# Three gathered neighbour sums of a graph network as products with a matrix of edge counts in bf16

## The reference

```python
# 1, attention (8 relations, 4 heads):
feat = einsum('ni,rhid->rnhd', h, conv_weights)
e = leaky_relu(el[type, src] + er[type, dst], 0.2)     # per edge and head
alpha = softmax of e over the edges with the same dst
x += segment_sum(alpha[..., None] * feat[type, src], dst) + h_bias
# 2, GCN (10 clusters): degrees count the edges and one more self loop
logits = D^-1/2 (A + I) D^-1/2 ((h + sum(cluster_emb)) @ W) + bias
x += h + softmax(logits) @ cluster_emb
# 3, GIN: edge network, then an MLP 256 -> 1024 -> 1024 -> 256 with layer norms
e = relu(edge_attr @ ee_w1 + ee_b1) @ ee_w2 + ee_b2
# with self loops, whose attributes are zero
agg = segment_sum(h[src] + e, dst)
x += relu(ln(h + MLP((1 + eps) * h + agg)) * bn_g + bn_b)
# 4, SAGE: mean over the in-edges
h = relu(ln(ln-and-relu of x) * gamma + beta)
x += (segment_sum(h[src], dst) / max(deg, 1)) @ W_l.T + b_l + h @ W_r.T
```

## Time and profile before

| | us |
|---|---|
| median of 3 runs | 4173.94 (4170.83 to 4174.08) |
| the profiled execution | 4168.64 |
| its span | 4166.8 |

### The profile page before, as it was taken

The page is one execution under the profiler, slowest core; times in us unless marked ns, Lnnn a source line. Parts: engine busy times, 40 slices in busy tenths (PEclk is TensorE's granted clock), DMA queues, the critical chain, the costliest instruction groups (busy, mean ns, idle before and its releaser), DMA issues.

```text
span 4166.8 us, 59236 instructions
## 1 busy us (share of the span) xinstructions
PE 3273.9 (79%) x16728; PEld 2258.8 (54%) x16728; DVE 2326.6 (56%) x4971; ACT 1189.8 (29%) x3540; POOL 1989.6 (48%) x2014
## 2 busy tenths in 40 slices
PE   3898388888868888887788888899999973666666
PEld 3444255555545554454777777555555542665556
DVE  6788577777664444446555555444444456555444
ACT  1222377778721111112111111233333322000000
POOL 0000477777307777772777777100000004777774
PEclk6899699999958889886899999999999986777767
DMA  4344333434211111111344444100000003333333
GB/s 99 118 152 142 109 107 108 107 108 108 56 45 36 17 17 17 17 16 44 111 113 114 114 114 113 45 5 5 5 5 5 5 12 95 102 102 101 102 102 101
DMA packets 216469, 301.43 MB, mean 72 GB/s; under 512 B 122598, under 2 KB 162715, under 8 KB 212251
## 3 DMA queue, kind: packets, MB, share of 16 engines
q0 software_dynamic: 88000, 200.32, 18.1%
q1 hardware_dynamic: 124027, 67.66, 6.4%
q10 hardware_dynamic: 4320, 31.95, 1.9%
HBM read 255.85 MB, written 43.93 MB: 72 GB/s over the span
## 4 chain that ended last, share of the span: by engine, by line
POOL 35%; PE 30%; DVE 13%; issue 13%; DMA 4%; ACT 3%; DVEq 1%; SPq 1%; ACTq 0%; POOLq 0%
POOL BG L406 14%; POOL SL L406 13%; PE PS L897 12%; POOL BG L416 7%; PE PS L723 3%; DVE SUMS L1112 3%; PE PS L608 3%; PE PS L765 3%; PE PS L746 2%; PE PS L721 1%; DVE OHB L1119 1%; PE PS L761 1%; PE PS L786 1%; ACT SL L565 1%; DMA BG<-rel_d 1%
## 5 line engine op out<-in xcount | busy, mean ns | idle before, releaser
L1248 DVE TENSOR_TENSOR SUMS<-SUMS,PS 128x256 f32 (+1 forms) x1750 | 709.0, 415 | 988.0 <-PE PS L746 363.7
L416 POOL DMA_INDIRECT BG<-feat_d,IDXST x500 | 484.4, 969 | 501.2 <-DMA feat_d<-SUMS 349.2
L406 POOL DMA_INDIRECT SL<-h_d,IDXS x500 | 502.8, 1006 | 289.1 <-issue 149.2
L406 POOL DMA_INDIRECT BG<-h_d,IDXS x500 | 491.7, 983 | 152.3 <-issue 148.0
L897 PE MATMUL PS<-BG,SL 128*128 128x512 f32 (+1 forms) x1440 | 533.0, 527 | 26.6 <-ACT SL L565 26.6
L765 PE MATMUL PS<-OHB,SL 128*128 128x128 f32 x2000 | 339.7, 328 | 248.1 <-DMA SL<-h_d,IDXS 202.9
L515 ACT ACTIVATE BG<-BG,SL 128x64 f32<-128x64 f32 x2000 | 482.0, 335 | 0.0
L765 PE MATMUL PS<-OHB,BG 128*128 128x128 f32 x2000 | 340.4, 329 | 179.7 <-DMA BG<-h_d,IDXS 131.1
L765 PEld LDWEIGHTS PS<-OHB,SL 128*128 128x128 f32 x2000 | 310.6, 236 | 281.8 <-issue 181.8
L765 PEld LDWEIGHTS PS<-OHB,BG 128*128 128x128 f32 x2000 | 308.1, 236 | 215.4 <-DVE SUMS L1248 128.3
L897 PEld LDWEIGHTS PS<-BG,SL 128*128 128x128 f32 x1440 | 271.8, 192 | 261.7 <-issue 211.7
(11 more groups left out here) (232 smaller groups left out, 4229.4 us busy)
## 6 DMA issues: line engine op xcount, KB each, us to landing
feat_d<-SUMS ACTq DMA_DIRECT2D x30, 1040.0 KB, 4.5
BG<-rel_d SPq DMA_DIRECT2D x100, 160.0 KB, 3.1
AL<-in_edge_attr_dram SPq DMA_DIRECT2D x100, 128.0 KB
BG<-feat_d,IDXST POOLq DMA_INDIRECT x500, 2.8
SL<-h_d,IDXS POOLq DMA_INDIRECT x500
BG<-h_d,IDXS POOLq DMA_INDIRECT x500
h_d<-BG SPq DMA_DIRECT2D x8, 640.0 KB, 3.3
BG<-in_L_gnn_w_dram SPq DMA_DIRECT2D x1, 4096.0 KB, 20.4
```

The costliest lines, as they stand in the source:

```text
L406: pool.indirect_dma_start(SLOTS[t // 10 % 2][:, t % 10, 0:width], None, table, bass.IndirectOffsetOnAxis(ap=IDXS[:, t:t + 1], axis=0),).th ...
L416: pool.indirect_dma_start(RING[:, t // NB % 3, t % NB, :], None, table, bass.IndirectOffsetOnAxis(ap=IDXST[:, t:t + 1], axis=0),).then_inc ...
L1248: return tt(a, a, v, ALU.add)
```

## The change

The neighbour sums of layers 2, 3 and 4 are computed as products with a dense matrix of edge counts, a_d, in HBM (3,840 sources by 4,352 columns, bf16, 33.4 MB). Columns 512 and up are destinations. Column t below 512 takes the edges of tile t that go to its first destination, since these alone can be shared with the tile before; after a product DVE adds such a held column t to column `BASE[t]`.

1. *Counts.* Two edges of a tile with the same source and destination must be written as one count. In layer 1's loop PE turns a broadcast column of KEY (source times 4096 plus relative destination) into the free quarter of the tile's bank, and DVE compares it with KEY and sums the matches into MULT (one instruction more a tile on each). `added` is now incremented by this instruction.
2. *The matrix.* POOL clears ZRO, SP writes zeros over a_d in 30 DMAs, one for every 15 tiles of layer 1. After layer 1's loop POOL issues 499 scatters (`TR = T - 1`; the last tile is padding only), each of 128 two-byte elements, one behind the other with no wait between them. Their landings are counted in four semaphores, for which SP waits before the first load from a_d.
3. *Edge network.* It runs alone, between layer 2's rows and its product, over all 125 groups of four tiles, with its own double buffers.
4. *Product of layer 2.* The rows of y are split into three bf16 parts (30 columns together), stationary; a_d streams in 5 column groups of 1,024 (the last of 256) by 30 source tiles, through 7 slots.
5. *Products of layers 3 and 4.* h is split into three bf16 parts of 256; a step (group, source tile) has 12 matmuls of 512 columns, or 6 of 256 in the last group. ACT casts, DVE subtracts, five tiles at a time. Turns and layer 4's self product stand between the steps of the first group. h3_d and y_d are gone, h2_d stays for the residual of the MLP.
6. *Places.* The parts and slots lie in BG, AL, SL and HSF. W1 is loaded after the first product, W2, W3 and the bias rows after the second.
7. Many single-use semaphores are merged into `dve_mark` and `pe_mark`.

The diff, cut to its core:

```diff
@@ SP @@
+            sp.wait_ge(s("zero_ready"), 1)
+            for t in range(NT):
+                sp.wait_ge(s("agg_ps"), 20 + 15 * t)
+                load(rows(a_d, t).rearrange("p (a n) -> p a n", a=2), bc(ZRO.unsqueeze(1), [P, 2, AD // 2]), "a_zero")
...
+            def adjacency(p, g, t):
+                n, (c0, w) = adj(p, g, t), GROUPS[g]
+                if n >= NR:
+                    sp.wait_ge(s("a_used"), n - NR + 1)
+                load(AR[p][n % NR][:, 0:w], a_d[t * P:(t + 1) * P, c0:c0 + w], f"a_in{n % NR}")
...
+            for k in range(4):
+                sp.wait_ge(a_set[k], 16 * len(range(k, TR, 4)))
+            sp.wait_ge(s("dve_mark"), DVE_MARKS["y_ready"])
+            adjacency_from(0, 0, every)
+            adjacency_from(1, 0, NR)
+            sp.wait_ge(s("a_used"), every)
             load(W1S, w1.rearrange("(c p) n -> p c n", p=P), "mlp_in")
...
+            sp.wait_ge(s("a_used"), 2 * every)
+            load(BR[0], row(b1, P), "mlp_bias")
+            load(W2S, w2.rearrange("(c p) n -> p c n", p=P), "mlp_late")
+            for v, a in ((BR[1], b2), (B3R, b3), (GNR, bn_g), (BNR, bn_b)):
+                load(v, row(a, P), "mlp_bias")
             load(W3S, w3.rearrange("(c p) n -> p c n", p=P), "mlp_late")
@@ POOL @@
-            gather(2, y_d, K)
...
-            gather(3, h2_d, D)
...
-            gather(4, h3_d, D)
+            pool.wait_ge(s("a_zero"), 16 * NT)
+            pool.wait_ge(s("dve_mark"), DVE_MARKS["adj_ready"])
+            for t in range(TR):
+                pool.indirect_dma_start(
+                    a_d.rearrange("n (w o) -> (n w) o", o=1), bass.IndirectOffsetOnAxis(ap=IDXST[:, t:t + 1], axis=0),
+                    VAL[:, t:t + 1], None,
+                ).then_inc(a_set[t % 4], 16)
@@ PE @@
-                last.then_inc(s("agg_ps"), 1)
+                turn(PS[:, bank, 3 * P:4 * P], bc(KEY[:, n:n + 1], [P, P]), P).then_inc(s("agg_ps"), 1)
...
+            def adjacent(p, g, t, lhs):
+                w = GROUPS[g][1]
+                if t == 0 and g >= 2:
+                    pe.wait_ge(s("d_free"), p * len(GROUPS) + g - 1)
+                rhs = adjacency_here(pe, p, g, t)
+                for part in range(3):
                     for c in range(2):
+                        for o in range(0, w, 512):
+                            m = min(512, w - o)
+                            last = pe.matmul(PS[:, 4 * (g % 2) + 2 * c + o // 512, 0:m], lhs(t, part)[:, c * P:(c + 1) * P],
+                                             rhs[:, o:o + m], start=(t == 0 and part == 0),
+                                             stop=(t == NT - 1 and part == 2))
+                last.then_inc(s("a_used"), 1)
...
+            for v in range(NE):
+                for k in range(4):
+                    hidden_sum(v, k)
+                    if k == 0 and v + 2 < NE:
+                        net_turn(v + 2)
+                    if k % 2 == 1 and v + 1 < NE:
+                        hidden(v + 1, k // 2)
@@ DVE @@
                     add = tt(a, a, PS[:, AGG_BANKS[n % 4], 0:3 * P].rearrange("p (a n) -> p a n", a=3), ALU.add)
                     add._wait_ge(s("added"), n + 10)
-                    add.then_inc(s("added"), 1)
+                    ts(SAME[:, n % 2, :], PS[:, AGG_BANKS[n % 4], 3 * P:4 * P], KEY[:, n:n + 1], 0.0, ALU.is_equal, ALU.add,
+                       accum_out=MULT[:, n:n + 1]).then_inc(s("added"), 1)
...
+            def neighbours(p, into, held, banks):
+                for g, (c0, w) in enumerate(GROUPS):
+                    dve.wait_ge(s("a_used"), adj(p, g, NT - 1) + 1)
+                    v = banks(g)
+                    if g == 0:
+                        step(cp(held, v[:, :, 0:512]))
+                    o = 512 if g == 0 else 0
+                    a = into[:, :, c0 + o - 512:c0 + w - 512]
+                    step(tt(a, a, v[:, :, o:w], ALU.add))
+                    dve.engine_nop().then_inc(s("d_free"), 1)
+                    for n in range(GR * g, min(GR * (g + 1), TR)):
+                        if n % 10 == 0:
+                            base = bases(n, 10)
+                        a = into[:, :, bass.ds(base[n % 10], 1)]
+                        step(tt(a, a, held[:, :, n:n + 1], ALU.add))
```

More of the change, by code:

```diff
@@ new lines, in adjacency, with adjacency_from @@
+            def adjacency(p, g, t):
[3 more added lines that the diff above has]
+                load(AR[p][n % NR][:, 0:w], a_d[t * P:(t + 1) * P, c0:c0 + w], f"a_in{n % NR}")
+            def adjacency_from(p, first, last):
+                for g in range(len(GROUPS)):
+                    for t in range(NT):
+                        if first <= g * NT + t < last:
+                            adjacency(p, g, t)
@@ new lines, in self_product, with h3_part @@
+            def self_product(t):
+                pe.wait_ge(s("n3_ht"), t + 1)
+                if t >= 2:
+                    pe.wait_ge(s("n3_done"), t - 1)
+                for c in range(2):
+                    last = pe.matmul(PS[:, 6 + t % 2, 0:D], HTR[:, t % 2, c, :], WLR[:, 1, c, :],
+                                     start=(c == 0), stop=(c == 1))
+                last.then_inc(s("n3_ps"), 1)
+            def h3_part(t, part):
+                return HIMID[:, t, part, :] if part < 2 else LO[:, t, :]
@@ L1283, in _, with edge_one_hot, bases @@
-            dve.wait_ge(s("f0_den"), 1)
+            def edge_one_hot(v):
+                k = slice(4 * (v % 2), 4 * (v % 2) + 4)
+                tt(OH[:, k, :], bc(IOTA[:, :].unsqueeze(1), [P, 4, P]),
+                   bc(DREL[:, 4 * v:4 * v + 4].unsqueeze(2), [P, 4, P]), ALU.is_equal).then_inc(s("oh_ready"), 1)
+            def bases(first, n):
+                _, base = nc.values_load_multi_w_load_instructions(
+                    BASE[:, first:first + n], engines=[DVE], min_val=0, max_val=N,
+                    skip_runtime_bounds_check_because="clamped to N when it was computed")
+                return base
@@ new lines, in _ @@
+            dve.engine_nop().then_inc(s("ys_ready"), 1)
+            neighbours(0, ACC[0:K3, 1:2, :], VBK.unsqueeze(1),
+                       lambda g: PS[0:K3, 2 * (g % 2):2 * (g % 2) + 2, :].rearrange("p (c a) n -> p c (a n)", c=1))
+            dve.wait_ge(s("pe_mark"), PE_MARKS["f1_tp"])
+            for i in range(2):
+                step(dve.tensor_reduce(Z[:, 15 * i:15 * i + 15, :],
+                                       PS[:, 4 + i, 0:15 * K3].rearrange("p (t a k) -> p t k a", t=15, a=3), AX, ALU.add))
@@ L1324, in _ @@
+            step(tt(Z, Z, Y, ALU.add))
             step(tt(Z, Z, bc(DG[:, :].unsqueeze(2), [P, NT, K]), ALU.mult))
```

623 lines of the change are left out of this document (329 added, 294 removed).

## The result

The changed kernel took 3850.11 us (median of four runs, 3833.78 to 7338.08) where the kernel before took 4174.01 (4170.83 to 4177.25) beside it: ratio 0.921, 95% interval 0.918 to 0.924. On a further chip, in a later series, it took 3846.47 (3843.31 to 3850.89) against 4171.75, ratio 0.922 (0.920 to 0.923). One run in eight took 7338 us; it has no trace, nothing explains it, and it is left out of the ratio. The forecast was 3680 us with a range of 3600 to 3840: the direction was right, the time 170 us too short and 10 us outside the range.

The account below looks back on a forecast made before the run. Three of the four neighbour sums were taken as bound by POOL's issue of gathers, the MLP by TensorE. The terms summed to -497 us: 4168.6-497+5 = 3677, say 3680 us, range 3600 to 3840.

Parts of the forecast that it names:

- Attention sum: Layer 1's loop: the added comparison makes DVE the bound at 1.41 us a tile, +67 us, POOL's start +3.
- Between: Stretch after the attention sum: three small copies and larger memsets, +2 us on 104.
- Scatters and edge network: After the attention sum, side by side: 499 scatters at 1.31 us set the end at 658 us; edges take 495.
- rival 1: Scatters run at the pace of landing, 2.8 us each instead of 1.31: +744 us, 4421 us in all; chance 0.06.
- rival 2: Scatters at 1.5 to 2.2 us each; at 1.8, +245 us, 3925 us in all; chance 0.07.
- rival 5: Edges and scatters run one after the other, both asking DMA queues for small packets: +440 us, 4120; chance 0.01.
- GCN product: Layer 2's product after the scatters: DVE's 499 held adds and 50 fetches set the end, 154 us (140 to 200).
- Softmax on the clusters: The softmax takes one more reduction: +1 us.
- GIN product: Layer 3's product: 350 us instead of 686.4, -336, with loads and DVE's held adds hidden.
- MLP: W2 can load only after the product, so DVE waits for five bias rows: +14 us (5 to 20).
- SAGE product: Layer 4's product, from ACT's last pass over the rows: 387 us instead of 681, -294.
- Rival 3: Products slower than 0.215 us a pass, by PE's clock or weight loads: +116 us at clock 0.85, 3795; chance 0.08.

Follow-up runs that it names:

- run 3672: No follow-up run: 3672 us is the forecast for the changed kernel's profiled run, 4168.6-497, without the 5 us added for the median of the runs; measured 3850.
- the run with two parts: Changed kernel with the lowest of three bf16 parts left out of the GIN and SAGE products: 3778.93 us, ratio 0.906.
- the last version: Changed kernel plus GCN held columns on TensorE, spread pads, four scatters out at most, twenty bases a fetch, reordered GIN/SAGE work: 3652.71 us, ratio 0.876.
- four out: Changed kernel with each scatter waiting for the landing of the one four before it: 3838.71 us, ratio 0.920.
- the four variants that ran there: Changed kernel without GCN held adds (4389.66 us), with fixed columns (4404.58), with twenty bases a fetch (4483.96), without counting (4547.84).

## Why the prediction was right in direction and wrong in size

Forecast for the profiled run 3672, measured 3850: 178 us to place.

- *Attention sum*: forecast +70, measured +58 (1197.4 against 1139.6). VectorE was the bound, as said, though busy for 85% of the stage (88% from the first add on), not over 90. The counting by itself is worth 51 to 54 us. In the pair below the comparison starts 0.47 us after its add and the next add 0.39 after the comparison: the comparison was priced well (0.36), but the add no longer costs the 0.58 that five dependent ones took the earlier trace rows, since the comparison need not wait for it: 0.86 us a pair where I had 0.94. That is 40 us over 500 tiles, and the loop from the first add took 670 us, 1.34 a tile, where 1.41 makes 705. But the forecast counted its 1.41 us a tile from the stage's start with 3 us ahead of it, while the first add comes only 26 us in (500.8 to 526.9; it was 20 before). So -35 and +23 make the -12: the stage came out nearly right because two errors went against each other. The accumulator's read is an instruction of its own (the first two lines are the adds of all 500 tiles, before and after):

```profile
L1229 DVE TENSOR_TENSOR SUMS<-SUMS,PS x500: 525/555/558, 521.5 to 1139.0; 128x384 f32 x167
L1330 DVE TENSOR_TENSOR SUMS<-SUMS,PS x500: 524/554/559, 526.9 to 1196.6; 128x384 f32 x167
...
1191.83 0.56 DVE L1330 TENSOR_TENSOR SUMS<-SUMS,PS 128x384 f32 x1
1192.30 0.34 DVE L1332 TENSOR_SCALAR_CACHE_REDUCE SUMS<-PS,SUMS 128x128 bf16<-128x128 f32 x1
1192.57 0.08 DVE L1332 DVE_READ_ACCUMULATOR SUMS<-PS,SUMS 128x1 f32 x1
1192.69 0.56 DVE L1330 TENSOR_TENSOR SUMS<-SUMS,PS 128x384 f32 x1
```

- *Between*: forecast +2, but the scatters, not this stretch, are on the path: -2.
- *Scatters and edge network*: 1.304 us a scatter (forecast 1.31), 499.5 us for the edges (495), both side by side and nothing of rivals 1, 2 and 5 on this chip. From the end of the last to the first load: 18 us, not 2.8, by the pads' one address, so 670.5 instead of 658: +12.
- *GCN product*, the step that failed: "499 held columns one by one ... I take 0.20, plus 50 fetches of bases at 0.45". Measured from the first load it is 266.8 us (1867.9 to 2134.7) instead of 154, +113: the adds 499 x (0.29-0.20) = 45, the fetches 50 x (1.72-0.45) = 64 (of each gap of 1.86, 0.14 belong to the add), the rest 4. The mechanism (VectorE sets the end) was right; both prices were wrong, and the range of 140 to 200 too narrow. The rows were misread twice. The pace of dependent instructions in the earlier trace rows was of fixed addresses, and the adds at a register's address in the same group stood at 0.38 for 0.28 long, so 0.10 from end to start: with 0.148 of length that is 0.25, nearer to the truth than the value I took. And the 0.87 us before L1203 was halved for half as many bases, though nothing in the trace said that a fetch scales; the runs show a fixed part, and ten bases cost twice what I had read for twenty. The row itself was typical (22.6 us of idle time in all 25 fetches of that loop, 0.90 each); why twenty bases stop VectorE for 1.53 us between the held adds is open.
- *Softmax on the clusters*: 48.3 against the forecast 46.6: +2.
- *GIN product*: forecast 350, measured 384: +34. A step is 2.59 us and the clock 1.0 in the middle groups, as forecast. What was called hidden was not: VectorE's held adds (73 us a group in the run with two parts, 2352.6 to 2426.0, not 37) leave 49 behind the last full group, so it ends 8 us after TensorE (2559.3, 2567.4). And in the first group TensorE stood 3.5 us at each block of five rows, waiting for ScalarE's last cast, as VectorE's second difference was queued behind five turned tiles that wait for TensorE. I had counted casts only ahead of the product. Behind three of these five waits, and in the group's first step, the granted clock was down too (0.50, which is 1.2 GHz, to 0.66), and a step took up to 5.3 us instead of 2.75, some 7 us in all. The tail of 8, the waits of 18 and these 7 make 33 of the 34 (below, the row with a colon is the busy time of one such step, with the clock third from its end).

```profile
2213.60 4.45 PE L859 MATMUL PS<-AL,BG 128*128 128x512 bf16 x12 [3.52 <-ACT BG L590]
...
2233.02 2.76 PE L859 MATMUL PS<-BG 128*128 128x512 bf16 x11 [3.52 <-ACT BG L590]
...
2270.19 5.30 PE L859 MATMUL PS<-AL,BG 128*128 128x512 bf16 x12 [3.53 <-ACT BG L590]
...
2270.20:2275.60 5.40, 5.40 (x14) 2.17 (x15) 1.49 (x1) 1.27 (x1) 0.00 (x0) 0.50 0.01 3
...
2564.02 2.62 DVE L1383 TENSOR_TENSOR SUMS<-SUMS,OHB 128x2 f32 x9 [2.48 <-issue]
2566.67 0.69 DVE L1377 TENSOR_TENSOR SUMS<-SUMS,PS 128x512 f32<-128x512 f32 x1
```

- *MLP*: forecast +14, measured 829.8 against 815.3 (2637.8 to 3453.1): right, with the wait where it was put, for the bias rows behind W2. The wait shows as 11 us only because VectorE was still at its held adds when the loads went out; from there to its first instruction of the MLP it is 19 us (2559.3 to 2578.3). So the tail of 8 us counted under GIN is not lost, since the loads ran beside it:

```profile
2559.32 0.33 SPq L294 DMA_DIRECT2D BG<-in_L_gnn_b_dram  x1
...
2578.32 0.88 DVE L1500 TENSOR_TENSOR OHB<-SUMS,PS 128x256 f32<-128x256 f32 x2 [10.97 <-DMA BG<-in_L_gnn_bn_b_dram]
```

- *SAGE product*: forecast 387, measured 417: +30, by the same tail (7.5 us, given back in the last version), 17 us of waits for ScalarE's copies of the turned self rows (L664) in its first group, and some 5 us that no row is named for; the start, 22 us after ScalarE's pass began, was as forecast.
- *Tail of the kernel*: +2.

The terms add up to the 178, within rounding. Rival 3 (clock) cost little: the GCN product ran at 0.67, but TensorE waited in it, and elsewhere the 7 us behind GIN's casts hung on it, and a part of SAGE's unnamed 5 (0.71 in the first 5.5 us of its first group). Rival 5 was priced at +440 us, but by its own terms the edges behind the scatters add all their 495. For rival 1 the run with one scatter at a time gives the price: 2.51 us, not 2.8, so 4442, and the unchanged pace at four out shows that the kernel is clear of that case. The Trainium skill (DMA: Bandwidth & Descriptors, Specifications) has transfers below 512 B done as a read-modify-write; scatters of 2 bytes at 1.304 us show nothing of it in POOL's pace, as weighed, and whether the 0.13 us of writes to one address are that, no run here shows.

## What to carry to other kernels

When a loop leaves the queue that bound it, price the small serial chain that remains instruction by instruction, from rows with the same kind of address and the same number of registers fetched; a chain of 499 tiny adds made a stage of 88 us one of 243. Work "hidden" at 37 of 78 us must be checked at double its price, and its remainder behind the last group counts in full, unless a load runs beside it. VectorE's large instructions beside POOL's scatters slow the scatters, which matters when these are on the path. Pads that all write to one address are not free: give each its own.

## What the hardware showed unexpectedly

- A dependent VectorE add of 30x1 at a fixed address stands 0.182 us from the next, at a register's address 0.29; a fetch of ten bases stops the engine for 1.24 or 2.48 us, one of twenty for 1.53.
- 122 writes of 2 bytes to one HBM address held back the completion of their scatter by 16 us; to different addresses a whole scatter lands 2.1 us after POOL starts it.
- Beside six VectorE instructions of 2.85 us each (128x2560, bf16 from f32), a scatter occupied POOL for 2.55 us instead of 0.96.
- On one chip the kernel before took 4712 us (4692.75 to 4717.74 in seven runs). In the traces of the four variants that ran there, every other engine crept while POOL scattered: this row, of the one without held adds, has 670 us with TensorE busy for 76, where the same stretch elsewhere held nearly the whole edge network.

```profile
1358.10:2028.60 670.50, 75.91 (x255) 46.10 (x253) 72.20 (x242) 23.35 (x41) 517.09 (x498) 0.50 0.02 1
```

The largest waits of TensorE and of VectorE in that stretch name no work, and the edge network began at 2077, after the last scatter: rival 5 in the flesh, though not by the DMA queues of small packets, whose share is 2%.

```profile
PE PS L889 <- issue: 364.6, 24, 15.3
DVE BG L1170 <- issue: 271.3, 17, 16.0
```

What holds the other engines' issue on that chip while POOL scatters stays open; no later run fell on it, and no other trace here shows it. The scatters are not all of it: the kernel before, which has none, was 540 us slower there too, and the attention loop took 825 us instead of 670.
